# Query projections of an attention layer in six fp32r products instead of two fp32 ones

## The reference, cut to what matters

```python
x = x + tanh(g_ffn[1]) * _L1_ffn_ref(_layernorm(x), wg, w1, v1, w2)      # 32 experts, width 96
h = _layernorm(x)
q = h @ Wq + bq          # 256 -> 16 heads x 128 = 2048 columns
k = ctx @ Wk + bk        # 4 key heads x 128
v = ctx @ Wv + bv
q = rmsnorm(q) * qn_w;  k = rmsnorm(k) * kn_w
p = softmax(q k^T / sqrt(128) + mask)     # per head, 256 x 256
x = x + tanh(g_xattn[2]) * ((p v) @ Wo)
```

## Time and profile before

| | |
|---|---|
| time, median of 3 runs | 1437.56 us (1437.15 to 1441.52) |
| the profiled execution: time | 1442.4 us |
| its span, first to last instruction | 1440.7 us |
| PE busy | 1323.7 us, 92% |
| DVE busy | 1013.1 us, 70% |
| ACT busy | 811.2 us, 56% |
| POOL busy | 676.8 us, 47% |
| the loop of the first mixture | about 150 to 338 us |
| the attention of layer 2, from its first projection | 345.7 to about 640 us |
| PE busy from 400 to 600 us | 200 of 200 us |

### The profile page before, as it was taken

One profiled execution on the slowest core, in us unless ns is written; L12 is line 12 of the kernel. 1 busy time (PEld: TensorE's weight loads), 2 busy tenths in 40 slices (PEclk: granted clock), 3 DMA queues, 4 the chain that ended last, 5 costly groups with the idle time before them and its releaser, 6 DMA issues.

```text
span 1440.7 us, 23168 instructions
## 1 busy us (share of the span) xinstructions
PE 1323.7 (92%) x7154; PEld 1084.6 (75%) x7154; DVE 1013.1 (70%) x2205; ACT 811.2 (56%) x2019; POOL 676.8 (47%) x699
## 2 busy tenths in 40 slices
PE   5988999998899999989999799999988899999994
PEld 3546888886577777767888478888877788888783
DVE  8787565656877877855556577878888777877753
ACT  6744222224565666674222577676777677776362
POOL 1010555553343434426551246655557767665443
PEclk9997999999999999999999999999999999999997
DMA  6221555562100000011110394000020001014283
GB/s 223 95 88 55 157 172 183 165 189 86 69 8 23 8 16 1 2 44 38 45 44 21 135 335 133 1 1 31 30 81 31 30 30 59 31 49 166 88 296 103
DMA packets 68497, 121.00 MB, mean 84 GB/s; under 512 B 6900, under 2 KB 36232, under 8 KB 67883
## 3 DMA queue, kind: packets, MB, share of 16 engines
q1 hardware_dynamic: 66139, 115.51, 24.6%
q0 software_dynamic: 2256, 4.24, 0.8%
HBM read 82.56 MB, written 39.12 MB: 84 GB/s over the span
## 4 chain that ended last, share of the span: by engine, by line
PE 66%; DVE 14%; issue 7%; ACT 6%; POOL 4%; DMA 2%; SPq 1%; POOLq 0%; ACTq 0%; DVEq 0%
PE ps L1360 9%; PE ps L1488 8%; PE ps L1461 8%; PE ps L1439 7%; PE ps L1506 6%; PE ps L1304 6%; PE ps L1374 5%; PE ps L1471 4%; PE ps L1165 3%; PE ps L1450 3%; PE ps L1320 3%; POOL urs L919 2%; DVE usum L2861 2%; DVE nmax L2886 1%; DMA rows_out<-tile_y,tile_to 1%
## 5 line engine op out<-in xcount | busy, mean ns | idle before, releaser
L926 POOL TENSOR_TENSOR probs<-probs,prec 128x512 f32<-128x512 f32 x192 | 202.1, 1053 | 323.3 <-DVE prec L2893 323.1
L2085 ACT ACTIVATE probs<-ps,nmax 128x256 f32<-128x256 f32 x384 | 178.6, 471 | 216.5 <-DVE nmax L2886 216.3
L1461 PE MATMUL ps<-k_feat,q_feat 128*128 128x256 f32 x768 | 198.4, 381 | 1.9 <-ACT q_feat L2076 1.9
L1488 PE MATMUL ps<-probs_t,v_tok 128*128 128x256 f32 x768 | 199.4, 383 | 0.2 <-ACT ob L2104 0.2
L919 POOL TENSOR_TENSOR urs<-uve,neg_half 128x4 f32<-128x4 f32 x136 | 136.9, 1007 | 53.5 <-DVE uve L2862 42.8
L2886 DVE TENSOR_REDUCE nmax<-ps 128x2 f32<-128x512 f32 x192 | 131.6, 686 | 30.5 <-PE ps L1461 27.6
L1461 PEld LDWEIGHTS ps<-k_feat,q_feat 128*128 128x128 f32 x768 | 136.9, 191 | 16.2 <-issue 2.7
L1471 PEld LDWEIGHTS ps<-ident,probs 128*128 128x128 f32 x768 | 93.2, 141 | 67.4 <-issue 40.9
L1488 PEld LDWEIGHTS ps<-probs_t,v_tok 128*128 128x128 f32 x768 | 132.0, 192 | 10.9 <-issue 0.8
L1471 PE MATMUL ps<-ident,probs 128*128 128x128 f32 x768 | 117.1, 275 | 23.6 <-ACT probs_t L2094 23.3
L2094 ACT ACTIVATE probs_t<-ps 128x512 f32<-128x512 f32 x192 | 115.2, 600 | 0.9 <-PE ps L1471 0.9
(11 more groups left out here) (409 smaller groups left out, 3619.2 us busy)
## 6 DMA issues: line engine op xcount, KB each, us to landing
rows_in<-zero_rows SPq DMA_DIRECT2D x3, 5200.0 KB, 35.3
tile_w<-in_l3f_w SPq DMA_DIRECT2D x21, 385.5 KB, 7.3
w<-in_l1f_w SPq DMA_DIRECT2D x24, 256.0 KB, 5.3
spread_w<-we_dram SPq DMA_DIRECT2D x16, 384.0 KB, 3.8
kv_cross<-kv_out SPq DMA_DIRECT2D x20, 256.0 KB
kv_first<-kv_out SPq DMA_DIRECT2D x16, 256.0 KB
spread_w<-we_dram SPq DMA_DIRECT2D x16, 256.0 KB, 3.9
w<-in_l2f_w SPq DMA_DIRECT2D x8, 512.0 KB
```

The lines of the kernel that those rows point to most:

```text
L926: pool.tensor_tensor(p3, p3, spread(prec[g % 3][:, :], [P, TB, S]), ALU.mult)\
L1461: mm = pe.matmul(ps[g % 2][:, j * S:(j + 1) * S], q_feat[:, h, j * P:(j + 1) * P], k_feat[:, kv, :], start=True, stop=True)
L1488: mm = pe.matmul(ps[6][:, 0:S], v_tok[:, tb, kv * P:(kv + 1) * P], probs_t[g % 2][:, tb, :], start=tb == 0, stop=tb == TB - 1)
L2085: ins = act_e.activation(probs[g % 4][:, j, :], ps[g % 2][:, j * S:(j + 1) * S], ACT.Exp, bias=nmax[g % 3][:, j:j + 1], accum_out=psums[g ...
```

## The change

The query projection of layer 2 takes six fp32r matmuls of 128x512 for a unit instead of two fp32 ones: for each half of the features the tokens' high part times the weights' high part, the tokens' high part times the weights' low part, and the tokens' low part times the weights' high part.

- The weights' parts are made in iterations 7 to 10 of the mixture's loop: a copy on ACT into `wq_first` and a subtraction on DVE into `w_high["q"]`, each of 128x1024. The loops of ACT and DVE are cut in three for it.
- `copy_late` writes the tokens' high part `h_query` (the same memory as `h_feat`) instead of `h_feat`.
- DVE makes the tokens' low part from `ps[4]` and `h_query`, four operations of 128x512 at the ends of steps -8, -4, -3 and -2. `turn_late(b)` now also waits for the low part of b - 1, and a projection for that of its batch.

```diff
@@ attention, PE
                     else:
-                        pe.wait_ge(part_out, FIRST_LN * B + b + 1)
-                        weights, x_in_, at_ = (wsets[0]["q"],), h_feat, b * S + j * P
+                        pe.wait_ge(h_split, B + b + 1)
+                        part = (slice(None), slice(None), slice(b * S + j * P, b * S + (j + 1) * P))
+                        low = source_low(b)[:, :, j * P:(j + 1) * P]
+                        whole = h_query[part]
+                        terms = [(whole, wq_first), (whole, w_high["q"]), (low, wq_first)]
@@ turn_late, PE
                     pe.wait_ge(part_out, k * B + b)
+                if b and k == FIRST_LN:
+                    pe.wait_ge(h_split, B + b)
@@ copy_late, ACT
-                    act_e.activation(part(h_feat, b), two(bank), ACT.Copy).then_inc(part_out, 1)
+                    act_e.activation(part(h_query, b), two(bank), ACT.Copy).then_inc(part_out, 1)
@@ packed_experts, ACT
-                with act_e.Fori(1, f.E // 2) as i:
+                first, end = QUERY_PIECES
+                with act_e.Fori(1, first) as i:
+                    four(i)
+                act_e.wait_ge(at["l2x"]["w_in"], 16 * 8)
+                with act_e.Fori(first, end) as i:
+                    four(i)
+                    act_e.activation(query_piece(wq_first, i), query_piece(wsets[0]["q"], i), ACT.Copy)\
+                        .then_inc(scalar_hi, 1)
+                with act_e.Fori(end, f.E // 2) as i:
                     four(i)
@@ packed_experts, DVE
+                with v.Fori(first, end) as i:
+                    st.enter(i - first, 4)
+                    four(i)
+                    v.wait_ge(scalar_hi, i - (first - 3))
+                    raw = query_piece(wsets[0]["q"], i)
+                    v.tensor_tensor(query_piece(w_high["q"], i), raw, query_piece(wq_first, i).bitcast(F32), ALU.subtract)\
+                        .then_inc(query_lo, 1)
+                    st.leave(end - first)
@@ late_norms, DVE
+                if k == FIRST_LN and t in (-8, -4, -3, -2):
+                    b = max(0, t + 5)
+                    v.wait_ge(part_out, k * B + b + 1)
+                    v.tensor_tensor(source_low(b), ps[4][:, :].rearrange("p (k s) -> p k s", k=KB),
+                                    h_query[:, :, b * S:(b + 1) * S].bitcast(F32), ALU.subtract).then_inc(h_split, 1)
```

More of the change, by code:

```diff
@@ L239, in build @@
         x_tok = sb("x_tok", [P, NT, D])
+        with ExitStack() as a:
+            h_query = sb("h_query", [P, KB, NTOK], F32R, where=a)
         h_feat = sb("h_feat", [P, KB, NTOK])
@@ L272, in build @@
             wo_raw = sb("wo_raw", [P, HEADS, D], where=a)
+        with ExitStack() as a:
+            wq_first = sb("wq_first", [P, KB, 2048], F32R, where=a)
         with ExitStack() as a:
@@ L407, in build @@
                 mask = sb("mask", [P, TB, S], where=a2)
+            with ExitStack() as a2:
+                query_last = sb("query_last", [P, KB, S], F32R, where=a2)
             zf = sb("zf", [P, KB * S], where=a)
@@ L1430, in project @@
                         pe.wait_ge(s["src_ready"], src_at[b] + i + 1)
-                        weights, x_in_, at_ = (w_high[what], w_low[what]), src_e4[i], j * P
-                    else:
-                        pe.wait_ge(part_out, FIRST_LN * B + b + 1)
-                        weights, x_in_, at_ = (wsets[0]["q"],), h_feat, b * S + j * P
+                        part = (slice(None), slice(None), slice(j * P, (j + 1) * P))
+                        terms = [(src_e4[i][part], w) for w in (w_high[what], w_low[what])]
+                    else:
+                        pe.wait_ge(h_split, B + b + 1)
[3 more added lines that the diff above has]
+                        terms = [(whole, wq_first), (whole, w_high["q"]), (low, wq_first)]
                     if f.kinds[b] == "cross" and f.kinds[b - 1] == "self":
@@ L1437, in project @@
                     for kb in range(KB):
-                        for q, w in enumerate(weights):
-                            mm = pe.matmul(ps[f.bank(p)][:, :], x_in_[:, kb, at_:at_ + P],
+                        for q, (x_in_, w) in enumerate(terms):
+                            mm = pe.matmul(ps[f.bank(p)][:, :], x_in_[:, kb, :],
                                            w[:, kb, n * HALF:(n + 1) * HALF],
-                                           start=kb == 0 and q == 0, stop=kb == KB - 1 and q == len(weights) - 1)
+                                           start=kb == 0 and q == 0, stop=kb == KB - 1 and q == len(terms) - 1)
                     mm.then_inc(s["proj_ready"], 1)
@@ L1945, in _ @@
                 act_e.wait_ge(s[f"w2_in{c}"], 16)
-                act_e.activation(w2_hi[c][:, 0:1, :], w2[c][:, 1:2, :], ACT.Copy).then_inc(first_hi, 1)
+                act_e.activation(w2_hi[c][:, 0:1, :], w2[c][:, 1:2, :], ACT.Copy).then_inc(scalar_hi, 1)
             early(1)
@@ L2727, in packed_experts @@
                 four(0)
-                with v.Fori(1, f.E // 2) as i:
+                first, end = QUERY_PIECES
+                with v.Fori(1, first) as i:
                     st.enter(i - 1, 4)
                     four(i)
-                    st.leave(f.E // 2 - 1)
+                    st.leave(first - 1)
+                with v.Fori(first, end) as i:
[6 more added lines that the diff above has]
+                    st.leave(end - first)
+                with v.Fori(end, f.E // 2) as i:
+                    st.enter(i - end, 4)
+                    four(i)
+                    st.leave(f.E // 2 - end)
                 def add(c):
```

15 lines of the change are left out of this document (12 added, 3 removed).

## The result

The changed kernel takes 1433.78 us (median of 20 runs, 1429.66 to 1438.90), the kernel before 1438.74 us in 20 runs of the same session. The ratio is 0.9968, with a 95% interval of 0.9957 to 0.9978: 4.6 us less (0.0032 x 1438.74). The forecast was 5.6 less, a ratio of 0.9961, which lies inside the interval. One of the 20 runs of the kernel before took 6861.56 us; no trace of it exists, and without it the median of before is 1438.54.

What follows compares the result with a forecast made beforehand. PE's own work was taken to bound the layer's middle. Span 1440.7 - 8.6 + 3.0 = 1435.1 us; from the median, 1437.56 - 5.6 = 1432.0 us, with 1429.0 to 1436.0 for 8 in 10.

Steps and rivals of the forecast that it cites:

- The cheaper projection: Layer 2's full stage: a query unit falls from 1.72 to 1.39 us, and 26 units save 8.6 us.
- layer 3's price: Same-shape fp32r matmuls in layer 3's attention: 0.232 us each, so six take 1.39 us.
- DVE-bound rival: Full stage: DVE becomes the bound, the 8.6 us are gone and 3.0 remain, 1440.6 us; chance 0.07.
- the one of dearer matmuls: Query projection: a unit takes 1.55 instead of 1.39 us, gain 4.4, time 1436.2; chance 0.05.
- The mixture: Weights' parts on ACT and DVE in the mixture's iterations 7 to 10: counted as costing 0.
- the 2.0 that I had set against them: Mixture: 2.0 us free between a unit's low part and its down products, against 1.28 for DVE's subtraction.
- The start: Layer's start: four low parts on DVE delay the first exponential by 3.0 us; 3.8 with 0.84 for each part.
- the rival of an absorbed start: Layer's start: it absorbs the low parts, loss 0 to 1 us, time 1429.0 to 1430.0; chance 0.15.
- The clock: TensorE's clock at the start: the first fall sits on matmuls with slack, no change counted.
- the sign that I had named for being wrong: Profile after: PE waits between 385 and 595 us, a clock below 1.00 after 356, or a start 5 us late.
- The rival that it costs more (0.12): Start: the clock falls once more, one or two L1165 groups take 1.72 us more each, 1433.7 to 1435.4; chance 0.12.
- The sum: Whole kernel: 8.6 us saved, 3.0 lost, 5.6 off the median 1437.56, giving 1432.0 us.

Runs made afterwards that it cites:

- four_products: Changed kernel without the third product (tokens' low part times weights' high part), the low parts and their waits; four fp32r matmuls per unit: 0.9885 of the kernel before.
- weights_only: Kernel before with the weights' high and low parts made in the mixture's iterations 7 to 10 but read by nobody; two fp32 projections kept: ratio 0.9989.
- tokens_only_again: The `tokens_only` file run a second time, in another session: 1.0013 of the kernel before, first exponential 30.68 us after the first key projection.
- banks_gaps: Changed kernel with batches' tokens in banks 4, 6, 7, 4, no PE wait for low parts, and low parts moved behind the maxima on DVE: 0.9957 of before.
- after_filled: Changed kernel plus unused identity products on PE, 14 before the first query projection, 17 before a key unit's first transposes: 0.9960 of the kernel before.
- tokens_only: Kernel before plus the tokens' low parts (unused) and both new PE waits; two fp32 projections on rounded tokens: ratio 1.0033, first exponential at 32.35 us.
- banks_gaps_free: `banks_gaps` with PE's transposes also no longer waiting for ACT's copy of the batch before: 0.9945 of the kernel before.
- gaps: Changed kernel with low parts moved behind the maxima in DVE's list, one step later, all still in bank 4: 0.9967 of the kernel before.
- free_filled: `banks_gaps_free` plus a filling of 32 unused identity products on PE ahead of the first query projection: 0.9945 of the kernel before.

## Why the prediction was right

- **The cheaper projection**: 26 x 0.33 = 8.6 us forecast, 8.3 measured. A unit takes 1.39, as layer 3's price said; two steps take 7.88 instead of 8.21, where key units pass 8.39 and 8.33 instead of 8.65 and 8.66, and the last interval is 8.00. PE's rows show no wait in it, so the DVE-bound rival and the one of dearer matmuls are out. `four_products` shows that the first wasn't far: 0.46 us less of PE in a unit, and PE begins to wait.
- **The mixture**: 0 forecast, 0 measured (`weights_only`). DVE's pieces took 1.97 on the mean instead of 1.28, and three of four were over the 2.0 that I had set against them. By my own working that would have cost up to 0.3 us each; it cost nothing because I had also counted the whole piece as delay, where DVE's wait for `gated` takes up most of it (0.62 of 2.31 left) and 1.57 us stay free. The zero holds, but two errors in its working met.
- **The start**: 3.0 us forecast, 3.13 measured. Against the markers of before, each moved on by the 0.23 us of the later mixture, the transposes of batch 2 are late by 1.27 (forecast 1.2), those of batch 3 by 2.07 (1.86), the sum by 3.14 (3.0), so the rival of an absorbed start is out. The links are those of the forecast: the copy of batch 1 late by 0.59 (0.65), then each low part behind its copy and each set of transposes behind the low part. What is more than forecast came in along those links. `tokens_only_again` gives 3.15 for the tokens' side alone, `banks_gaps` 0.06 with both places changed.
- **The clock**: in the two profiled executions of the changed kernel it fell on matmuls with slack, and `after_filled` shows that it cost nothing there. It was low for longer than before, though, 349.6 to 356.4 us against 350.9 to 354.4, so the sign that I had named for being wrong, a clock below 1.00 after 356 us, came about by 0.4 us without meaning anything. The rival that it costs more (0.12) did not come about here, but it exists: the first `tokens_only` shows the 1.7 us. The Trainium skill, "TensorE: Matmul & The Clock Gate", "Why this matters for your kernels", warns of long idle gaps, and I had held that rule against the added waits of 1.2 and 0.7 us, which are not long; in `tokens_only` no pause of PE in the start was longer than 2.09 us before the fall, and the clock fell.
- **The sum**: -8.3 + 3.1 = -5.2 in the layer, against -5.3 in the trace, -4.6 (-3.2 to -6.2) in the times and -5.6 forecast. Of the 1.8 us between the forecast 1432.0 and the measured 1433.78, 1.2 come from its base, the median of three runs (1437.56) instead of twenty (1438.74). One bound was added up wrongly: four low parts of 0.84 us instead of 0.68 make the loss 3.6, not 3.8.

What to do with it: `banks_gaps_free` with or without the filling is 0.55% faster than the kernel before (0.9945), where the change as made is 0.32% faster. The intervals of the two overlap, so the ratios alone don't rank them; the start in the traces does, 27.70 and 27.50 us against 30.66.

## What to carry to other kernels

Splitting a product into cheaper ones moved work here to the engines that make the parts, and what that cost was decided at the pipeline's start, where nothing covered it: follow copy, part and release of the bank as one chain there, step by step, and the sum can come out to tenths of a microsecond, as it did here. An operation that only reads a buffer in order to make a side product should neither stand ahead of others' work in its engine's list nor hold a buffer that the next round needs, and it takes both edits together, since here the one alone gave less than half and the other alone made it worse. Before counting on the full gain of PE time taken out, ask from which size on the next engine sets the pace: here two products fewer would have been worth 5 us less than PE's arithmetic.

## What the hardware showed that I had not expected

- DVE's subtraction of two 128x1024 operands in SBUF took 1.22 us while POOL stood still, and 2.07 to 2.31 us beside an operation on POOL. The three slow ones end 1.08 or 1.09 us behind the end of the POOL instruction that was running when they started: 290.80 behind 289.71 (288.10 + 1.61), and in the same way 274.07 behind 272.99 and 306.43 behind 305.35. So they ran as if they had begun only when POOL was done. The 128x512 subtraction with one operand in PSUM took 0.69 us in all four places at the start. The Trainium skill, "SBUF — State Buffer", "Who interferes with whom", says that a DVE instruction with two SBUF inputs and a GpSimd one that reads SBUF exclude each other, the second waiting until the first is done; the three rows agree. No run here took POOL's work away on purpose, but over the ten executions that make these pieces the same four meet POOL at different moments: 20 of the 40 found an instruction of POOL's running, took 2.06 to 2.31 us and ended 1.08 or 1.09 us behind its end; the other 20 found none and took 1.22. The same piece, the second, took 2.31 in the changed kernel and 1.22 in `four_products`. And a high part of POOL's that began within a piece took longer than the 1.04 us of the row at 322.45: 2.06 us at 271.31 in `gaps`, ending 0.90 us behind the end of the piece.
- PE's clock fell to 0.50 at the start in 12 of the 14 profiled executions, all but `after_filled` and `free_filled`, and in four of them a second time before the full stage. It is not always the same instruction that it meets: the same kernel had it on a query projection at 353.27 and, in another execution, on a key projection at 357.54. What it cost depended on what it met: nothing there, 1.7 us on the key projection.
